# Sums of sixteen states' products by accumulating DMAs, and the router and the zero fill moved into the scan

## The reference

```python
def mamba_mixer(x, ...):                       # x: (2, 2048, 256); d_inner 512, d_state 16
    xp, z = jnp.split(x @ in_proj_w.T, 2, axis=-1)
    xc = jax.nn.silu(conv4(xp) + conv_b)       # causal, 4 taps
    x_dbl = xc @ x_proj_w.T
    dt = softplus(x_dbl[..., :16] @ dt_proj_w.T + dt_proj_b); Bm, Cm = ...
    def step(h, ts):
        dt_t, B_t, C_t, u_t = ts
        h = h * jnp.exp(dt_t[..., None] * A) + (dt_t * u_t)[..., None] * B_t[:, None, :]
        return (h, jnp.einsum('bds,bs->bd', h, C_t))      # the sum over 16 states
    y = ys + xc * D
    return (y * silu(z)) @ out_proj_w.T
xn = _layernorm(x)
s = xn + mamba_mixer(rmsnorm(xn)); s = s + silu(rmsnorm(s) @ mlp_w1.T) @ mlp_w2.T
g = silu(moe_top2_of_8(xn))                    # softmax gate, relu MLP 256 -> 1024 -> 256
return x + s * g
```

## Time and profile before

| | us |
|---|---|
| runs | 1621.5, 1621.36, 1628.53 (median 1621.5) |
| profiled execution | 1619.38, of which the span 1617.5 |
| busy in the span | PE 1332.7, DVE 1258.3, POOL 1179.3, PEld 954.6, ACT 890.5 |
| mean granted TensorE clock | 0.91 |
| first scan, first scan of block 1, last stretch | 90.8, 299.7, from 1540 |

### The profile page before, as it was taken

The page is one execution under the profiler, slowest core; times in us unless marked ns, Lnnn a source line. Parts: engine busy times, 40 slices in busy tenths (PEclk is TensorE's granted clock), DMA queues, the critical chain, the costliest instruction groups (busy, mean ns, idle before and its releaser), DMA issues.

```text
span 1617.5 us, 17492 instructions
## 1 busy us (share of the span) xinstructions
PE 1332.7 (82%) x5158; PEld 954.6 (59%) x5158; DVE 1258.3 (78%) x1571; ACT 890.5 (55%) x1948; POOL 1179.3 (73%) x608
## 2 busy tenths in 40 slices
PE   3845382789989899988988988989998998879977
PEld 2632120567667666766576756766676766656546
DVE  7179975388978898788878996788898887886844
ACT  4333443366565756575657756565766464554632
POOL 3425888576798779886798777777798679796840
PEclk8567886899989999989999999999999999988989
DMA  9614543656366545755365635755385637554650
GB/s 329 236 52 146 168 154 118 216 174 215 125 212 248 193 143 180 269 177 184 132 235 183 234 126 179 252 197 196 124 306 181 213 111 267 199 192 151 219 174 27
DMA packets 124607, 300.64 MB, mean 186 GB/s; under 512 B 14408, under 2 KB 29136, under 8 KB 114016
## 3 DMA queue, kind: packets, MB, share of 16 engines
q1 hardware_dynamic: 109632, 263.47, 48.2%
q0 software_dynamic: 8736, 26.22, 4.7%
q10 hardware_dynamic: 6144, 9.83, 1.7%
HBM read 259.75 MB, written 39.71 MB: 185 GB/s over the span
## 4 chain that ended last, share of the span: by engine, by line
PE 44%; issue 14%; POOL 13%; DVE 9%; ACT 6%; DMA 4%; SPq 0%; DVEq 0%; ACTq 0%; POOLq 0%
PE prod L935 36%; DVE state L1313 6%; POOL dbu L667 5%; PE ysum L984 4%; DMA xs<-slot_x 3%; POOL slot_x L654 3%; POOL hxc L683 3%; PE prod L940 1%; PE prod L1119 1%; ACT state L743 1%; PE prod L1120 1%; DVE hxc L1281 1%; DMA late<-slot_y,slots 1%; ACT late L901 1%; ACT L743 1%
## 5 line engine op out<-in xcount | busy, mean ns | idle before, releaser
L1313 DVE TENSOR_TENSOR_SCAN state<-state,carry,dbu 128x512 f32<-128x512 f32 x512 | 657.9, 1285 | 205.5 <-ACT state L743 187.0
L667 POOL TENSOR_TENSOR dbu<-dtu,bb 128x1024 f32<-128x1024 f32 x256 | 612.4, 2401 | 82.6 <-DVE state L1313 81.8
L683 POOL TENSOR_TENSOR hxc<-hxc 128x1024 f32<-128x1024 f32 x155 | 366.3, 2363 | 220.0 <-DVE hxc L1281 219.7
L743 ACT ACTIVATE state<-dt,par 128x512 f32<-128x512 f32 x512 | 353.5, 692 | 95.6 <-DVE hxc L1281 81.2
L1281 DVE TENSOR_TENSOR hxc<-state,cb 128x512 f32<-128x512 f32 x512 | 353.8, 691 | 36.0 <-DVE state L1313 0.5
L935 PE MATMUL prod<-late 128*128 128x256 f32 x1136 | 282.7, 407 | 43.1 <-issue 30.1
L935 PEld LDWEIGHTS prod<-late 128*128 128x128 f32 x1136 | 236.6, 211 | 91.8 <-issue 54.9
L935 PE MATMUL prod<-xsT,late 128*128 128x256 f32 (+1 forms) x1280 | 268.1, 363 | 17.0 <-issue 6.9
L984 PE MATMUL ysum<-hxc,ident 128*128 128x512 f32 x404 | 208.6, 642 | 69.1 <-DVE hxc L1281 41.4
L935 PEld LDWEIGHTS prod<-xsT,late 128*128 128x128 f32 x1280 | 225.1, 194 | 65.9 <-issue 28.4
L741 ACT COPY carry<-state 128x1 f32<-128x1 f32 x384 | 61.2, 159 | 241.0 <-DVE hxc L1281 234.1
(11 more groups left out here) (165 smaller groups left out, 1192.5 us busy)
## 6 DMA issues: line engine op xcount, KB each, us to landing
bb<-bc_rows SPq DMA_DIRECT2D x256, 256.0 KB, 5.8
cb<-bc_rows SPq DMA_DIRECT2D x256, 256.0 KB, 4.3
late<-moe SPq DMA_DIRECT2D x40, 1028.0 KB, 4.9
late<-moe SPq DMA_DIRECT2D x40, 1024.0 KB, 5.8
slot_x<-xc POOLq DMA_DIRECT2D x18, 512.0 KB, 10.8
xs<-slot_x SPq DMA_DIRECT2D x31, 256.0 KB, 6.3
slot_y<-ys ACTq DMA_DIRECT2D x31, 256.0 KB, 5.3
late<-x SPq DMA_DIRECT2D x12, 512.0 KB, 8.7
```

The costliest lines, as they stand in the source:

```text
L667: nc.gpsimd.tensor_tensor(dbu[:, v % 3, :, :], dtu[:, n % 2, 2 * h:2 * h + 2, :], b, ALU.mult).then_inc(dbu_ready, 1)
L683: nc.gpsimd.tensor_tensor(hxc[:, to, :, :], hxc[:, to, :, :], hxc[:, piece, :, :], ALU.add).then_inc(summed, 1)
L743: nc.scalar.activation(state[:, k % 2, :], dt[:, (2 * n + h) % 3, k % 2, :], ACT.Exp, scale=par[:, P_ALOG + col(k):P_ALOG + col(k) + 1]).t ...
L1313: nc.vector.tensor_tensor_scan(state[:, c, :], state[:, c, :], dbu[:, v % 3, c, :], carry[:, n % 2, col(k):col(k) + 1], ALU.mult, ALU.add) ...
```

## The change

- `GROUPS`: blocks 1 to 6 have one group of 16 a half, block 7 one of 16 and then 8, 2, 2, 1, 1, 1, 1. That makes 204 adds and 52 groups on PE.
- `ADD` is a DMA of 512 KB issued by GpSimd, from SBUF to SBUF, that adds the unit's product to the group's first buffer. Before it GpSimd waits for the unit's products and for the landing of the group's add before it (`sum_made`). Four semaphores `summed` take turns by group.
- `HX` is 7, and the product of unit v waits for the add of unit v-6 or for a group's use by PE of 7 units before. `LATER` puts `ADD` three steps behind on GpSimd (one before) and `ACC` eight behind on PE (four before).
- The prologue has `TX` and `LG` of groups 0 to 3 alone; groups 4 to 7 are at steps 1, 4, 7 and 10. DVE's token statistics are interleaved with the conv of block 0. `R_AT` is 13. The scatter runs from step 22 to step 60.
- The zero fill is issued by SyncE, one DMA of 512 KB at each of steps 1 to 18. The loads for the first expert are an event of their own, `FETCH`, at step 63 on SyncE, rows ahead of weights; `M_FROM` is 66.
- `STEPS_C` is some 2 to 3 steps later; in block 0 `YE0` and `YE1` are at step 35.

```diff
-GROUPS = [((1,) * NS,) * 2] + [((4,) * 4,) * 2] * (NB - 2) + [((4,) * 3 + (1,) * 4, (2,) * 2 + (1,) * 12)]
-HX = 5
+GROUPS = [((1,) * NS,) * 2] + [((NS,),) * 2] * (NB - 2) + [((NS,), (8, 2, 2, 1, 1, 1, 1))]
+HX = 7
+ADDED = 8
...
-STEPS_C = {"YE0": 38, "YE1": 38, "LOADN": 67, "Z0": 41, "Z1": 45,
-           "YE2": 70, "YE3": 70, "Z2": 71, "Z3": 73, "OUT0": 77, "OUT1": 79, "RMS": 81, "RCP": 82, "NORM": 82,
+STEPS_C = {"YE0": 41, "YE1": 41, "LOADN": 69, "Z0": 43, "Z1": 47,
+           "YE2": 73, "YE3": 73, "Z2": 74, "Z3": 76, "OUT0": 80, "OUT1": 82, "RMS": 84, "RCP": 85, "NORM": 85,
...
-FIRST = """A.LOADX A.XR A.TR0 A.TR1 R.TX00 R.TX01 L.L1 L.L2 L.L3 A.IN0 A.IN1 L.L4 L.L5 L.L6 L.L7 L.ROOT L.ZERO
- A.CV0a A.CV0b A.CV0c A.TH0 A.IN2 A.CV1a A.CV1b A.CV1c A.TH1 A.IN3 A.SL0 R.LG0 A.CV2a A.CV2b A.CV2c A.TH2 A.SL1
- A.CV3a A.CV3b A.CV3c A.TH3 A.SL2 A.SL3 L.XN A.XD A.BOUT A.DT0 A.DT1 A.DT2 A.DT3 R.TX10 R.TX11 R.LG1 A.SPE A.SPL
- R.TX20 R.TX21 R.LG2 R.TX30 R.TX31 R.LG3 A.DTA0 A.DTU0 A.DTA1 A.DTU1 R.TX40 R.TX41 R.LG4 R.TX50 R.TX51
- R.LG5 R.TX60 R.TX61 R.LG6 R.TX70 R.TX71 R.LG7"""
-R_AT = 5
+FIRST = """A.LOADX A.XR A.TR0 A.TR1 R.TX00 R.TX01 L.L1 L.L2 A.IN0 A.IN1 A.CV0a A.CV0b A.CV0c A.TH0 L.L3 A.IN2
+ A.CV1a A.CV1b A.CV1c A.TH1 A.SL0 A.IN3 R.LG0 L.L4 A.CV2a A.CV2b A.CV2c A.TH2 A.SL1 L.L5 A.CV3a A.CV3b A.CV3c A.TH3 A.SL2 A.SL3
+ L.L6 L.L7 L.ROOT L.XN A.XD A.BOUT A.DT0 A.DT1 A.DT2 A.DT3 R.TX10 R.TX11 R.LG1 A.SPE A.SPL R.TX20 R.TX21 R.LG2
+ R.TX30 R.TX31 R.LG3 A.DTA0 A.DTU0 A.DTA1 A.DTU1"""
+R_AT = 13
+R_FIRST = 4
...
-M_FROM, M_TO = 62, NK - 38
+M_FROM, M_TO = 66, NK - 38
...
-LATER = {"act": {"R": 1, "M": 1, "C": 1, "A": 1}, "dve": {"M": 1, "C": 1, "A": 0}, "pool": {"Y": 1, "A": 1},
-         "pe": {"Y": 4}, "sp": {"M": 2}}
+LATER = {"act": {"R": 1, "M": 1, "C": 1, "A": 1}, "dve": {"M": 1, "C": 1, "A": 0}, "pool": {"Y": 3, "A": 1},
+         "pe": {"Y": 8}, "sp": {"M": 2}}
...
+    for g in range(R_FIRST, NB):
+        at = R_AT - 3 * (NB - g)
+        out[at] += [("R", "TX%d0" % g, None), ("R", "TX%d1" % g, None)]
+        out[at + 2].append(("R", "LG%d" % g, None))
...
+    for z in range(Z_ROWS // (NT * P)):
+        out[1 + z].append(("R", "ZERO", z))
     for t in range(AT):
-        out[R_AT + 9 + t * 3 // 2].append(("R", "SC%d" % t, None))
+        out[R_AT + 9 + t * 5 // 4].append(("R", "SC%d" % t, None))
...
+            if n == 0 and name in ("YE0", "YE1"):
+                at = NS * 2 + 3
...
+    out[M_FROM - 3].append(("R", "FETCH", None))
...
+        def sum_made(eng, v):
+
+            q = Y_UNIT[v][0]
+            eng.wait_ge(summed[q % 4], 16 * sum(1 for u in range(v + 1) if Y_UNIT[u][0] % 4 == q % 4 and Y_UNIT[u][1]))
...
+                elif kind == "R" and name == "FETCH":
+                    sp.wait_ge(scattered, 16 * 2 * AT)
+                    load_rows(0)
+                    load_first(0)
+                    load_second(0)
+                    load_rows(1)
+                elif kind == "R" and name == "ZERO":
+                    if i == 0:
+                        sp.wait_ge(consts, CONSTS)
+                    sp.dma_start(slot_x[i * ZROWS:(i + 1) * ZROWS, :].rearrange("(p t) d -> p (t d)", p=P),
+                                 zeros).then_inc(zero_out, 16)
...
                     pool.wait_ge(hc_ready, 2 * i + 2)
                     if Y_UNIT[i][1] > 1:
-                        pool.wait_ge(summed, adds_before(i))
-                    nc.gpsimd.tensor_tensor(hxc[:, to, :, :], hxc[:, to, :, :], hxc[:, piece, :, :],
-                                            ALU.add).then_inc(summed, 1)
+                        sum_made(pool, i - 1)
+                    pool.dma_start(flat3(hxc[:, to, :, :]), flat3(hxc[:, piece, :, :]), accum_op=ALU.add
+                                   ).then_inc(summed[Y_UNIT[i][0] % 4], 16)
```

More of the change, by code:

```diff
@@ L77, in m_work @@
     return ["UP%d" % u for u in range(2 * size(i))] + ["MT"] + ["DN%d" % r for r in range(size(i))] + ["NEXT"]
-M_FROM, M_TO = 62, NK - 38
+M_FROM, M_TO = 66, NK - 38
 D_VECTOR = 5
 D_STEPS = [{"GA": M_TO + 1 + 7 * g, "MX": M_TO + 11 + 7 * g} for g in range(5)] + [
-    {"GA": NK + 2, "MX": NK + 16}, {"GA": NK + 10, "MX": NK + 36}, {"GA": NK + 16, "MX": NK + 54, "FI": NK + 59}]
+    {"GA": NK + 2, "MX": NK + 16}, {"GA": NK + 10, "MX": NK + 36}, {"GA": NK + 16, "MX": NK + 56, "FI": NK + 61}]
 COST = {"UP": 4, "MT": 1, "DN": 9, "TR": 1, "IN": 4, "XD": 8, "DT": 2, "Z": 4, "OU": 8, "T1": 1,
@@ L109 @@
 FIRST_UNIT = {q: v for v, (q, j, size) in enumerate(Y_UNIT) if j == 0}
-def adds_before(v):
-    return sum(1 for u in range(v) if Y_UNIT[u][1])
 def y_buffers():
@@ L126, in y_buffers @@
         if j:
-            back.append((2 * v + 4, buf, ("summed", adds_before(v) + 1)))
+            back.append((2 * v + ADDED, buf, ("summed", v)))
         if j == size - 1:
-            back.append((2 * v + 6, table[FIRST_UNIT[q]][0], ("y_acc", q + 1)))
+            back.append((2 * v + ADDED + 2, table[FIRST_UNIT[q]][0], ("y_acc", q + 1)))
     return table
@@ L198, in steps @@
     later = LATER.get(engine, {})
-    return [(k, e) for k, q, e in sorted((k + later.get(name[:2] if kind == "C" else kind, later.get(kind, 0)), q, (kind, name, i))
+    return [(k, e) for k, q, e in sorted((k + later.get(name[:2], later.get(kind, 0)), q, (kind, name, i))
                                          for q, (k, kind, name, i) in enumerate(EVENTS))]
@@ L408, in mamba_moe @@
         carried = sem("carried")
-        summed = sem("summed")
+        summed = [sem("summed%d" % i) for i in range(4)]
         y_acc = sem("y_acc")
@@ L602, in do @@
                 elif kind == "M":
[L603 to L609, removed]
+                    if name == "MT" and i < TILES - 1:
                         read_out(sp, ("M", "UP%d" % (2 * size(i) - 1), i))
@@ L672, in do @@
                     form(i // 2 + 2)
[L673 to L677, removed]
                 elif kind == "Y" and name == "ADD":
@@ L979, in do @@
                     if Y_UNIT[v][1]:
-                        pe.wait_ge(summed, adds_before(v) + 1)
+                        sum_made(pe, v)
                     else:
@@ L1276, in product @@
                     if what and what[0] == "summed":
-                        dve.wait_ge(summed, what[1])
+                        sum_made(dve, what[1])
                     elif what:
@@ L1299, in chore @@
                         norm(NT, AT)
-                    elif name != "ZERO":
+                    else:
                         token_stats(int(name[1]))
```

## The result

The changed kernel takes 1898.5 us (median of 4, 1884.8 to 1901.3) against 1622.0 us: 1.168 times the time of before, 95% interval 1.161 to 1.174. The forecast of 1551 was far off and outside its range; rival (1), the chain of sums, came closest, with 1733, and is 165 us under the measured time.

A forecast was written before the change was run, and what follows sets the result against it. It took DVE, at a ceiling of 89.5% busy, plus waits to bound blocks 1 to 7, and GpSimd before block 1. 1619.4 - 20 (start) - 50 (steady) = 1549, plus 2 for the median: 1551 us; own range 1525 to 1575, over the cases 1505 to 1670.

The forecast's parts named there:

- rival (1): Blocks 1 to 7: the serial chain of sums sets the pace at 7 us an add; 134 us lost, 1733; chance 0.24.
- The add's latency: GpSimd's DMA adds: issue to landing takes 5.5 us, bounds 2.9 and 8.0, under the 5.9 allowed.
- 1 us for queueing: Part of the 5.5 us for a DMA add: 1 us of queueing amid other traffic.
- the slack of 12 us: GpSimd's adds in a group of 16: 14 latencies may exceed 14 units by 12 us.
- the threshold of 5.9 us: GpSimd's adds: latency up to 5.9 us fits the slack in units of 5.05 us.
- its sign: Sign that the chain of sums sets the pace: halves of equal length near 15 latencies, GpSimd idle before each issue.
- Rival (2): Blocks 1 to 7: the DMA engines saturate; 1634 by share, 1599 by bytes, 1616 between the two; chance 0.15.
- Steady gain of 50 of 91 us: Blocks 1 to 7: with less summing on PE and GpSimd, DVE waits less; 50 us won of at most 91.
- The end: zero, 3 us either way: Block 7's small last groups and steps 2 to 3 later: order, not work; zero, 3 us either way.
- Prologue and START: Before block 1: first scan at 66 us, block 1 at 280 instead of 299.7; 20 us gained, bounds 8 and 27.
- The issue: GpSimd's issue of an adding DMA: 0.531 us as for a plain one, 1.1 us if it needs twice the descriptors.

The follow-up runs named there:

- no_adds: The changed kernel with its 204 DMA adds and the waits for sums left out (sums incomplete): 1620.8 us.
- two_chains: The changed kernel with two accumulators for each group of over two units, even and odd units added separately: 1684.1 us, ratio 1.040.
- order_only_no_adds: Kernel of before with only the new prologue, router and first-load order, and GpSimd's 155 adds left out (sums incomplete): 1603.8 us.
- no_adds_old_steps: The changed kernel without adds, with the old steps for a block's output and the old delays on PE and GpSimd: 1578.8 us.
- order_only: New prologue, router, zero fill and first-load order alone; groups, buffers, output steps and GpSimd's own adds as before: 1602.5 us, ratio 0.988.
- two_chains_old_c: The changed kernel with two accumulators per group and the old `STEPS_C`: 1698.9 us.
- order_pool_zero: The new order alone on the kernel of before, but with the zero fill issued by GpSimd in the prologue: 1604.1 us, ratio 0.989.

## Why the prediction failed

**The add's latency**, the failed step. "I take ... 5.5 us" was right as a median: 5.6. The data part was right too: 2.78 us for an add against 1.43 for a copy of the same bytes, nearly double. A reduction at half the rate of a copy is what the Trainium skill states ("Collectives: The Full Stack", Part 3, the bandwidth ceiling); the trace agrees. The fit for one DMA that the prediction takes from the Trainium skill ("DMA: Bandwidth & Descriptors", where it stands in the section "Anatomy of one DMA") gave an estimated 4.4 us with a second read; the quickest add, 4.5 us, agrees with it. Three things were wrong with the use of the 5.5 us. First, a chain adds latencies up, so the mean counts, and the mean link is 7.3 us. An add waits 1.45 us for its first packet or, in 37% of cases, over 3 us. I put "1 us for queueing" on every add from the landing of the B and C loads, which sit in SyncE's own queue. The 80 weight loads of 1 MB are what stands in the way of most late adds: without them 4% are late. Second, 0.5 us from landing to the next issue was left out. Third, the slack of 12 us, on which the threshold of 5.9 us rests, is there once in a half, and every link of 7.3 us in a unit of 5.05 takes 2.2 us of it: six links use it up, and a half has fourteen. Then PE stands at its `ACC` with ACT behind it (17.8 us in one wait). The changed kernel less no_adds is the price: 278 us.

**Rival (1)** had the right mechanism and a size of 134 us. With the measured link of 7.3 us for L its formula gives halves of 16 x (7.3 - 0.86) = 103 us; measured are 108.8. The halves are not of equal length, as its sign would have them: the second of a block takes 102 us in the mean, as the formula says, the first 115 (99.6 and 114.6 in the rows above). Why the first halves take more was not traced to one cause.

**Rival (2)**, capacity: the share rose from 0.57 to 0.85, the upper end of the forecast's 0.75 to 0.85, yet two_chains moves nearly the same bytes in 214 us less. It was not the pace. Late landings are contention all the same, in a serial chain.

**Steady gain of 50 of 91 us.** Wrong, and not only by size. The prediction expected less summing on PE and GpSimd to shorten DVE's waits. GpSimd's adds cost nothing before (order_only_no_adds). PE's 49 groups, with two buffers more, are worth 25 us when steps and delays are old and no adds are made (no_adds_old_steps). Even there the scans of blocks 1 to 7, from the start of the first to that of the last, take 1227 us, 11 less than before, not 91 less: the scan still waits 125.9 us for ACT, against 145.6 in order_only. That ACT in turn waits for PE results in list order, and that less PE work does not remove this, is a reading, not shown by a run of its own. PE does not save the full 101 us either: its busy time in no_adds is 1281.0 us, 52 less than before. The groups themselves take 117.8 us instead of 208.6, 91 less, and all other work on PE 39 more, beside a mean granted clock of 0.88 instead of 0.91. In the changed kernel PE is busy 1341 us, where the forecast looked for 1230.

**"The end: zero, 3 us either way"**, and nothing at all for the later delays. Without adds, all of them together cost 42 us, 10 of it in the tail, which has no scan beside it. For the 27 us of the delays the cause was not traced; PE's sums eight steps late stand in the same list as everything else. The 42 us can't simply be taken off the changed kernel, since sums that land late need the late steps (two_chains_old_c).

**Prologue and START.** First scan at 68.0 against 66 forecast, block 1 at 268.5 against 280: gain 31 us against 20. I kept too much for SyncE's zero fill (3 us, none measured in order_pool_zero). The stall went otherwise than forecast: I left 3 us of it ahead of block 1, and in the changed kernel 6.9 and 3.1 us stand in its third unit, behind ACT. Counted at the ninth scan of block 1 the gain is still 31 us. What the term left out is that some of it is given back in blocks 1 to 7, 17 us in the profiled execution of order_only; where, beyond its 7.7 us stall, stays open.

**The issue.** 0.88 us against bounds of 0.53 and 1.1: inside.

## What to carry to other kernels

Where an asynchronous transfer is a link of a serial chain, its mean latency under the traffic of the kernel is the pace, and one bulk load on another queue can double a link; look for the largest DMA that can be in progress, not for the median of similar ones. Break the dependence (two accumulators gave back 214 of 278 us) before counting on slack. Before work is taken off an engine, leave it out in an experiment: here GpSimd's adds were hidden, and fewer groups on PE with more buffers were worth 25 us without adds, so the offload had at most that to win.

## What the runs showed of the hardware

- An accumulating DMA of 512 KB from SBUF to SBUF landed in 4.5 us at best, a copy in 2.9. GpSimd's issue took 0.88 us for the one, 0.585 for the other. The first packet came 1.45 us after the issue of an add when nothing was in its way.
- An add issued behind a 1 MB load (784.98 in the changed kernel) got no packet through for 5.3 us; 37% of the adds had their first packet over 3 us after the issue. With the load cut into 128 KB DMAs the share was 17%, with light loads 4%.
- `form` is recorded with 2.66 us on GpSimd when it follows an add's issue at once, and with 2.40 otherwise. It then starts 0.6 us after the issue's start, within the issue's 0.88 us: both end 3.27 us after that start, as 0.88 and 2.40 one after the other would. The two records overlap, and `form` is not slower.
- PE's mean granted clock in the scan of blocks 1 to 7 was 0.96 before, 0.92 in no_adds and 0.85 in the changed kernel, and the expert matmuls (L935 of before, 128x256 from `late`) went from 407 ns before to 426 in the changed kernel. The mean over a stretch mixes the levels of 1.2 and 2.4 GHz.
